# A graph convolution on Trainium2: one indirect gather for each step instead of one for each tile of edges, into fixed buffers

## The reference

```python
# graph part: two layers, with self loops appended to the edges
norm = dis[src] * dis[dst]                 # dis = 1/sqrt(number of edges into a node)
out  = segment_sum((h @ W)[src] * norm[:, None], dst) + b
h    = elu(out)
# mixing part: linear attention over all 6250 rows
q, k = elu(q) + 1, elu(k) + 1
out  = (q @ context) * 1 / max(q . k_sum, 1e-6);   context = k^T v per head
out  = out @ Wproj^T + bproj
x = x + gnn(xn) + mix(xn)
x = x + ffn(layernorm(x))                  # top 2 of 8 experts, gelu, 256 -> 1024 -> 256
```

## Time and profile before

| what | us |
|---|---|
| median of 3 runs | 3484.71 (3480.18 to 3488.33) |
| the profiled execution: its own time | 3488.13 |
| the profiled execution: span in the profile | 3486.4 |
| preparation, 0 to 128.2 | 128.2 |
| layer 0, 128.2 to 1331.3 | 1203.1 |
| dense stage, 1331.3 to 1465.4 | 134.1 |
| layer 1, 1465.4 to 2656.5 | 1191.1 |
| routing and feed-forward part, to the end | 829.9 |

### The profile page before, as it was taken

How to read it: one execution, slowest core, us unless ns; L and a number is a source line. 1 busy time by engine, 2 the same in 40 slices (tenths; PEclk the granted TensorE clock), 3 DMA queues, 4 the chain that set the end, 5 groups by cost and what they waited for, 6 DMA issues and landing times. The chain is left out here.

```text
span 3486.4 us, 52130 instructions
## 1 busy us (share of the span) xinstructions
PE 2318.2 (66%) x12513; PEld 1677.3 (48%) x12513; DVE 1795.5 (52%) x4307; ACT 665.9 (19%) x1375; POOL 2016.0 (58%) x2139
## 2 busy tenths in 40 slices
PE   2156666666666667435556565665668689999998
PEld 2033333443444435323333333333336579999998
DVE  7334444444444445424444444444555756667676
ACT  2200000000000004400000010010103634444343
POOL 2666666666666662566666666666663235555554
PEclk9867777777677778756665567666668789999999
DMA  5544444444444440356666666666661346546551
GB/s 135 176 127 129 132 134 132 132 131 133 131 131 130 131 122 37 108 162 187 178 183 185 185 186 186 185 185 184 183 187 42 128 142 201 166 111 186 143 144 22
DMA packets 202955, 506.69 MB, mean 145 GB/s; under 512 B 42393, under 2 KB 96570, under 8 KB 194538
## 3 DMA queue, kind: packets, MB, share of 16 engines
q0 software_dynamic: 121824, 335.79, 36.1%
q1 hardware_dynamic: 50926, 109.87, 8.8%
q10 hardware_dynamic: 30012, 58.67, 4.8%
HBM read 425.37 MB, written 81.50 MB: 145 GB/s over the span
## 5 line engine op out<-in xcount | busy, mean ns | idle before, releaser
L689 POOL DMA_INDIRECT rows<-rows_layer,srcs x1564 | 1532.8, 980 | 811.2 <-SPq L711 430.1
L740 DVE TENSOR_TENSOR acc<-acc,l_bank 128x256 f32 x1666 | 699.2, 420 | 1301.5 <-PE l_bank L753 554.7
L750 PE MATMUL l_bank<-rows,sel 128*128 x1666 | 578.2, 347 | 722.7 <-SPq L705 319.7
L750 PEld LDWEIGHTS l_bank<-rows,sel 128*128 128x128 bf16 x1666 | 199.3, 120 | 989.8 <-SPq L705 522.5
L752 PE MATMUL l_bank<-rows,sel 128*128 x1666 | 589.3, 354 | 8.9 <-issue 8.8
L753 PE MATMUL l_bank<-rows,sel 128*128 x1666 | 588.5, 353 | 5.5 <-issue 5.5
L1718 PE MATMUL ps_y<-whl,hhi 128*128 128x512 f32 x896 | 320.8, 398 | 0.0
L718 DVE TENSOR_TENSOR sel<-iota_n,dloc 128x512 bf16<-128x512 f32 x418 | 286.3, 685 | 19.2 <-issue 19.2
L1674 POOL DMA_INDIRECT out<-ys,g_sum x112 | 180.3, 1610 | 196.7 <-DVE ys L1630 167.9
L1589 ACT ACTIVATE hr<-ffn_bank,vec 128x256 f32<-128x256 f32 x448 | 212.8, 475 | 372.3 <-PE ffn_bank L1530 333.2
L1528 PE MATMUL ffn_bank<-xh,whl 128*128 128x256 f32 x896 | 252.7, 282 | 2.4 <-DVE xl L1604 2.4
(11 more groups left out here) (285 smaller groups left out, 3126.7 us busy)
## 6 DMA issues: line engine op xcount, KB each, us to landing
whl<-w_hi SPq DMA_DIRECT2D x32, 1024.0 KB
whl<-w_lo SPq DMA_DIRECT2D x32, 1024.0 KB
rows<-rows_layer,srcs POOLq DMA_INDIRECT x1564
w_qkv<-wide ACTq DMA_DIRECT2D x49, 335.0 KB
w_hi<-whi ACTq DMA_DIRECT2D x49, 335.0 KB
w_lo<-wlo ACTq DMA_DIRECT2D x49, 335.0 KB
rows_layer<-part SPq DMA_DIRECT2D x25, 384.0 KB, 2.4
rows_layer<-prep_mem SPq DMA_DIRECT2D x7, 1344.0 KB, 5.2
```

Source lines behind the costliest of these rows:

```text
L689: pool.indirect_dma_start(rows[:, (n + 1) % ROWS, :], None, table[layer], bass.IndirectOffsetOnAxis(ap=srcs[:, n:n + 1], axis=0)).then_inc ...
L740: v.tensor_tensor(to, to, step_bank(s), ALU.add).wait_op(sem(f"summed{layer}"), s + 1, "sem-ge").then_inc(sem(f"added{layer}"), 1)
L750: t.matmul(step_bank(s), sel[:, s % SELS, :], rows_flat[:, bass.ds(slot * DP, D)], start=True, stop=False).wait_op(sem(f"here{layer}"), t. ...
```

## The change

Each step gets a gather of its own, also when two steps share a tile. So step s always finds its rows in slot s % 32, and its slot semaphore has a value that is known when the program is built (`landed`). TensorE's matmuls get constant addresses and wait for the slot's semaphore themselves; its registers and `tiles_of` go. GpSimd waits for `summed` itself, for the step 31 before (s - ROWS + 1). SyncE has no work in the layers any more: `tiles_here` and `steps_until_free` go, with `here` and `freed`. In the preparation the sources are fetched per step like the destinations, by seven indirect gathers on GpSimd; of the three tables of words the blocks' is left. `srcs` has 896 columns instead of 782. VectorE's `step_add` and `blocks_of` stay as they are, but for the table's index.

```diff
-BEHIND, FREED_AT = 16, 8
...
-            word_i = sb(ph, "word_i", [P, 3, SG, 2], U16)
+            word_i = sb(ph, "word_i", [P, SG, 2], U16)
...
-                    full = ET // P * P
-                    sp.wait_ge(sem("copy_s"), 32)
-                    sp.dma_start(rows_i[:, 1, 0:SG - 1, :], e_src_rows[0:full, :].rearrange("(g p) w -> p g w", p=P)
-                                 ).then_inc(sem("rows_s"), 16)
-                    sp.dma_start(rows_i[0:ET - full, 1, SG - 1, :], e_src_rows[full:ET, :]).then_inc(sem("rows_s"), 16)
-                    sp.wait_ge(sem("word_i"), 6)
+                    sp.wait_ge(sem("word_i"), 2)
                     with nc.allow_non_contiguous_dma("small"):
-                        for k in range(3):
-                            sp.dma_start(tab_d[k, :, :].rearrange("(g p) w -> p g w", p=P), word_i[:, k, :, :]
-                                         ).then_inc(sem("word_d"), 16)
+                        sp.dma_start(tab_d[0, :, :].rearrange("(g p) w -> p g w", p=P), word_i[:, :, :]
+                                     ).then_inc(sem("word_d"), 16)
...
+                    pool.wait_ge(sem("copy_s"), 32)
+                    for g in range(SG):
+                        at = bass.IndirectOffsetOnAxis(ap=t_i[:, g:g + 1], axis=0)
+                        pool.indirect_dma_start(rows_i[:, 1, g, :], None, e_src_rows, at).then_inc(sem("rows_s"), 16)
...
-                        v.tensor_scalar(word_i[:, 0, :, k], t_i[:, :], 1.0, None, ALU.add).then_inc(sem("word_i"), 1)
-                        v.tensor_scalar(word_i[:, 1, :, k], b_s[:, :], float(D), None, ALU.mult).then_inc(sem("word_i"), 1)
-                        v.tensor_copy(word_i[:, 2, :, k], tb[:, :]).then_inc(sem("word_i"), 1)
+                        v.tensor_scalar(word_i[:, :, k], b_s[:, :], float(D), None, ALU.mult).then_inc(sem("word_i"), 1)
...
-                    t.wait_ge(sem("rows_f"), 2)
+                    t.wait_ge(sem("rows_f"), 1)
                     for g in range(SG):
-                        n = min(P, ET - g * P)
-                        ins = t.transpose(ps_src[:, g * P:g * P + n], rows_f[0:n, g, :], ident[0:n, 0:n])
+                        ins = t.transpose(ps_src[:, g * P:(g + 1) * P], rows_f[:, g, :], ident[:, :])
...
-                    a.wait_ge(sem("rows_s"), 32)
-                    n = ET % P
-                    a.activation(rows_f[:, 0:SG - 1, :], rows_i[:, 1, 0:SG - 1, :], ACT.Copy).then_inc(sem("rows_f"), 1)
-                    a.activation(rows_f[0:n, SG - 1, :], rows_i[0:n, 1, SG - 1, :], ACT.Copy).then_inc(sem("rows_f"), 1)
-                    for j, (lo, hi) in enumerate(((0, 4 * P), (4 * P, ET))):
+                    a.wait_ge(sem("rows_s"), SG * 16)
+                    a.activation(rows_f[:, :, :], rows_i[:, 1, :, :], ACT.Copy).then_inc(sem("rows_f"), 1)
+                    for j, (lo, hi) in enumerate(ROW_COLS):
...
-            for n in range(ET):
-                if n >= ROWS:
-                    pool.wait_ge(sem(f"freed{layer}"), n - ROWS + 1)
-                pool.indirect_dma_start(rows[:, (n + 1) % ROWS, :], None, table[layer],
-                                        bass.IndirectOffsetOnAxis(ap=srcs[:, n:n + 1], axis=0)
-                                        ).then_inc(sem(f"slot_{n % ROWS}"), 16)
-        def steps_until_free(n):
-            _, regs = nc.values_load_multi_w_load_instructions(
-                words[2:3, n + 1:min(n + FREED_AT, ET - ROWS) + 1, 0], engines=(SP_ENGINE,), min_val=1, max_val=STEPS,
-                skip_runtime_bounds_check_because="the first step of the next tile of edges")
-            return list(regs)
-        def tiles_here(sp, layer):
-            until = []
-            for n in range(ET):
-                sp.wait_ge(sem(f"slot_{n % ROWS}"), (n // ROWS + 1 + layer * -(-(ET - n % ROWS) // ROWS)) * 16)
-                sp.sem_inc(sem(f"here{layer}"), 1)
-                m = n - BEHIND
-                if 0 <= m < ET - ROWS:
-                    if m % FREED_AT == 0:
-                        until = steps_until_free(m)
-                    sp.wait_ge(sem(f"summed{layer}"), until[m % FREED_AT])
-                    sp.sem_inc(sem(f"freed{layer}"), 1)
+            for s in range(STEPS):
+                if s >= ROWS:
+                    pool.wait_ge(sem(f"summed{layer}"), s - ROWS + 1)
+                pool.indirect_dma_start(rows[:, s % ROWS, :], None, table[layer],
+                                        bass.IndirectOffsetOnAxis(ap=srcs[:, s:s + 1], axis=0)
+                                        ).then_inc(sem(f"slot_{s % ROWS}"), 16)
+        def landed(layer, s):
+            return (s // ROWS + 1 + layer * -(-(STEPS - s % ROWS) // ROWS)) * 16
...
-                words[1:2, s:min(s + LOADED, STEPS), 0], engines=(DVE_ENGINE,), min_val=0, max_val=(BLOCKS - 1) * D,
+                words[0:1, s:min(s + LOADED, STEPS), 0], engines=(DVE_ENGINE,), min_val=0, max_val=(BLOCKS - 1) * D,
                 skip_runtime_bounds_check_because="a step's tile is one of the step's number or less, by less than the blocks")
-            return list(regs)
-        def tiles_of(s):
-            _, regs = nc.values_load_multi_w_load_instructions(
-                words[0:1, s:min(s + LOADED, STEPS), 0], engines=(PE_ENGINE,), min_val=1, max_val=ET,
-                skip_runtime_bounds_check_because="a count of tiles, 1 to ET")
             return list(regs)
...
-        def step_sum(t, layer, s, here):
-            slot = t.snap(here & (ROWS - 1))
-            t.to_reg(slot)
+        def step_sum(t, layer, s, rows):
             if s < PSB:
                 t.wait_ge(sem(f"selected{layer}"), s // FOUR + 1)
             else:
                 t.wait_ge(sem(f"added{layer}"), s - PSB + 1)
-            t.matmul(step_bank(s), sel[:, s % SELS, :], rows_flat[:, bass.ds(slot * DP, D)], start=True, stop=False
-                     ).wait_op(sem(f"here{layer}"), t.to_reg(here), "sem-ge")
-            t.matmul(step_bank(s), sel[:, s % SELS, :], rows_flat[:, bass.ds(slot * DP + D, D)], start=False, stop=False)
-            t.matmul(step_bank(s), sel[:, s % SELS, :], rows_flat[:, bass.ds(slot * DP + 2 * D, D)], start=False, stop=True
+            part_of = [rows[:, s % ROWS, k * D:(k + 1) * D] for k in range(3)]
+            t.matmul(step_bank(s), sel[:, s % SELS, :], part_of[0], start=True, stop=False
+                     ).wait_op(sem(f"slot_{s % ROWS}"), landed(layer, s), "sem-ge")
+            t.matmul(step_bank(s), sel[:, s % SELS, :], part_of[1], start=False, stop=False)
+            t.matmul(step_bank(s), sel[:, s % SELS, :], part_of[2], start=False, stop=True
                      ).then_inc(sem(f"summed{layer}"), 1)
...
-        def tensor_steps(t, layer, between):
-            tiles = tiles_of(0)
+        def tensor_steps(t, layer, rows, between):
             for s in range(STEPS):
-                step_sum(t, layer, s, tiles[s])
-                if s % LOADED == 1 and s + LOADED - 1 < STEPS:
-                    tiles.extend(tiles_of(s + LOADED - 1))
+                step_sum(t, layer, s, rows)
                 if s < NT * TURN:
                     between(s // TURN, s % TURN)
...
-                @block.sync
-                def _(sp):
-                    tiles_here(sp, 0)
```

More of the change, by code:

```diff
@@ L38 @@
 TURN = 16
-BEHIND, FREED_AT = 16, 8
-assert ROWS > BEHIND and ROWS & (ROWS - 1) == 0 and PAD_DST + NT < 1 << 16 and BLOCKS * D < 1 << 16 and ET < 1 << 16
+assert PAD_DST + NT < 1 << 16 and BLOCKS * D < 1 << 16 and ET < 1 << 16
 HEADS, HD = 8, 32
@@ L108, in gps_layer @@
     e_src = dram("edges_src", [ET * P, 1], I32)
-    tab_d = dram("step_words", [3, SG * P, 2], U16)
+    tab_d = dram("step_words", [1, SG * P, 2], U16)
     table = [dram(f"rows_layer{i}", [n * P, DP], BF16) for i, n in enumerate((NT, 2 * PAIRS))]
@@ L154, in gps_layer @@
         dloc = sb(steps_ctx, "dloc", [P, SG * P])
-        srcs = sb(steps_ctx, "srcs", [P, ET], I32)
-        words = sb(steps_ctx, "words", [3, SG * P, 2], U16)
+        srcs = sb(steps_ctx, "srcs", [P, SG * P], I32)
+        words = sb(steps_ctx, "words", [1, SG * P, 2], U16)
         ctx_q = sb(steps_ctx, "ctx_q", [P, KC, D])
@@ L431, in _ @@
                     sp.dma_start(node[0:TAIL, NT - 1, :], x[(NT - 1) * P:N, :]).then_inc(sem("x_last"), 16)
-                    sp.wait_ge(sem("word_d"), 48)
+                    sp.wait_ge(sem("word_d"), 16)
                     sp.dma_start(words[:, :, :], tab_d).then_inc(sem("words"), 16)
@@ L789, in gps_layer @@
             rows = sb(ph, "rows0", [P, ROWS, DP], BF16)
-            rows_flat = rows[:, :, :].rearrange("p r d -> p (r d)")
             sel = sb(ph, "sel0", [P, SELS, P], BF16)
@@ L889, in between @@
                             ins.then_inc(sem("m_kv"), 1)
-                    tensor_steps(t, 0, between)
+                    tensor_steps(t, 0, rows, between)
                     t.matmul(ps_c[:, 0:D], zero[:, 0:P], zero[:, 0:D], start=False, stop=True, skip_group_check=True)
```

(5 more changed lines are left out.)

## The result

| | before | after |
|---|---|---|
| median of the runs, us | 3483.68 (3480.18 to 3488.33, 4 runs) | 3554.5 (3552.9 to 3557.97, 4 runs) |
| ratio to before, 95% interval | | 1.0204 (1.0186 to 1.0221) |
| span in the profile, us | 3486.4 | 3551.2 |

The kernel became 70.8 us slower. The forecast was slower by 131 us, with 3385 to 3660 us as the range. So the direction is right, the time lies in the range, and the step is little more than half of what was forecast.

A forecast was written before the change was run, and what follows sets the result against it. The bound was a chain with waits, GpSimd's gathers and late TensorE signals throttling each other. From 3488.1 us profiled, +130 for gathers and +1 for preparation gave 3619, a median of 3616 us; range 3385 to 3660.

The forecast's parts named there:

- The pace goes with the gathers, not the steps: Both layers: gathers keep 1.47 to 1.50 us each while a step shrinks from 1.49 to 1.39 us.
- 51 gathers a layer at 1.28 us, +130: GpSimd in both layers: each added gather costs its unstalled 1.28 us, +65 us a layer.
- The stalls stay what they are: GpSimd's waits on the full ring, 0.22 and 0.20 us per gather, keep their sum after the change.
- the relay: SyncE passing landings to TensorE and sums to GpSimd; removal taken as 0, at most 0.22 and 0.20 us per gather.
- TensorE's registers: 209 register loads of 0.987 us per layer plus address arithmetic; removal taken as 0, at most 0.25 us a step.
- The forecast's own sign: Profile after: 833 gathers per layer, first and last start some 1225 to 1250 us apart, stalls about 0.2 us each.
- The pace of 1.481 at the start of layer 0: Stretch with one gather per step, 200 / 135 us, taken for all 833 gathers: +60 us in layer 0.
- Two parties throttling each other: Layers: gathering GpSimd delays TensorE's signals, late sums fill the ring, GpSimd stops, signals get through; stalls 0.22 and 0.20 us.
- The 7 us that I read off: Layer 0: VectorE's add of 149.01 was read as 7 us behind its matmul.
- Preparation +1: Before the layers: seven more gathers against fewer stores and VectorE operations, +1 us, bounds -5 and +6.
- partial relief: Layers: the shorter chain shortens stalls, 1.37 us per step, -33 and -19, 3434 us; chance 0.20.
- No lateness any more: Layers: direct waits end GpSimd's full-ring stalls, 1.28 us a gather, -108 and -94, about 3284 us; chance 0.10.

The follow-up runs named there:

- before_again: The kernel before, unchanged, run again with a profile on a third chip, one without stalls: 3117.8 us.
- after_again: The changed kernel, unchanged, run again beside the kernel before on a chip without stalls: 3235.47 us, 1.0366 of before.
- gathers_782: The changed kernel with 782 gathers per layer again, spread over 833 steps, output wrong: 3098.06 us, 0.9931 of before.
- plain_loads: The changed kernel with each step's 128 rows loaded by a plain SyncE DMA of consecutive rows, no GpSimd gathers: 2582.0 us, chip with stalls.
- three_stores: The changed kernel with the table of words stored three times instead of once: 3535.39 us, where before took 3460.95.
- registers: The changed kernel with TensorE's register loads, address arithmetic and dynamic addresses put back, with two stores of words: 3238.48 us, 1.0379 of before.

## Why the prediction came out as it did

First the two comparisons of spans, from the first and last start of each layer's gathers (us):

| | chip of the result | chip without stalls (before_again, after_again) |
|---|---|---|
| preparation | -4.8 | -5.6 |
| layer 0, first to last gather | 1172.1 to 1208.2: +36.1 | 1004.9 to 1060.4: +55.5 |
| layer 0, behind the last gather | 30.8 to 25.6: -5.2 | 6.8 to 5.3: -1.5 |
| dense stage | 134.2 to 131.2: -3.0 | 132.9 to 137.2: +4.3 |
| layer 1, first to last gather | 1159.1 to 1206.9: +47.8 | 1006.3 to 1070.8: +64.5 |
| layer 1, behind the last gather | 31.3 to 25.3: -6.0 | 6.8 to 5.0: -1.8 |
| the rest | -0.2 | +3.5 |
| span | +64.8 | +118.9 |

- **The pace goes with the gathers, not the steps: right where nothing stalls.** gathers_782 took away 102 gathers, and 130 us went from the layers. With stalls it wasn't tried, and there 102 more gathers cost 84 us.
- **51 gathers a layer at 1.28 us, +130: right as the price of a gather, wrong as the whole.** Where GpSimd doesn't stall, the gathers cost +120 (55.5 + 64.5), 1.18 us each, and 1.28 us is the interval itself. On the chip of the result they cost +84.
- **The stalls stay what they are: the step that failed.** The forecast took 0 for the relay and 0 for TensorE's registers. The interval fell from 1.501 to 1.452 and from 1.484 to 1.451 us: over 832 gathers that is -40 and -28 us, and behind the last gather another -5 and -6. The bound given for it (the whole stall, 0.22 and 0.20 us a gather) held, and the true value is some 0.05 and 0.03 of it: about a fifth. The forecast's own sign, 1225 to 1250 us from first to last gather, failed with it, at 1208 and 1207. What part of the diff brought the relief isn't settled. Relay and registers were each put back, but only on chips without stalls, where neither moves the time by more than 6 us.
- **The pace of 1.481 at the start of layer 0 as the pace of the layer after: failed with it.** That stretch had one gather per step, but also the relay and the register loads; I used it as if only the ratio counted. The changed kernel runs 200 / 138 = 1.449 there.
- **Two parties throttling each other: right for that chip.** After the change finished sums still wait up to 31 us for their adds, and plain_loads shows the lateness gone without the gathers. The 7 us that I read off were the interval from one add to the next: the add of 149.01 is that of the sixth sum, 7.8 us behind it, and the eighth waits 24 us. But I took it for how a gathering GpSimd works. On three other chips GpSimd gathers without a stop and the signals are prompt, so the reading holds for the chip that it was taken from and is no rule.
- **Preparation +1: wrong in sign, inside its bounds.** -4.8 us, all of it from the stores (three_stores), and one of the two fewer would have done (registers). The seven new gathers cost nothing: their conversion starts at 37.92 us, where it had been 38.62. (The forecast's 44.4 us for that conversion was also added up too high: by its own terms it is 43.5 to 43.8, which makes the upper bound +5; nothing hangs on it.)
- **Of the rivals,** partial relief was the nearest: its mechanism, a shorter stall, is what happened, at 1.45 us and not at its 1.37, and so without its sign. "No lateness any more" came about as a property of a chip, and then the change costs more, not less: the kernel before isn't late either.

## What to carry to other kernels

When GpSimd issues indirect gathers one after the other, count them first: a 128-row gather took GpSimd 1.28 us here where it didn't stall, with 1536 bytes a row and with 512, and a scheme that makes addresses constant by gathering more often paid 1.18 us for each more where nothing stalled and 0.82 us where the gathers stalled. A price for a wait that two engines share (a stall per gather) shouldn't be carried over when the hand-over behind it changes; give the change in the hand-over a value between its bounds, not the end that says nothing happens. Pair a signal with its reader by counting steps, not by what stands next to each other in a timeline. And where a wait is far longer than the work it waits for, look at the same program on a second chip before explaining it by the program.

## What the runs showed of the hardware that was not expected

- The same program has two paces: 3461 to 3484 us in two groups of runs and 3118 to 3119 us in three, on other chips. For the kernel before, the spans differ by 370.3 us, and 368.6 of them lie between the first gather and the last add of the two layers; the part behind layer 1 takes 830.5 in both. The granted clock doesn't explain it: for the changed kernel it is 0.762 on the slower chip and 0.756 on the faster one.
- On the slower chips TensorE's completion signals reach VectorE up to 31 us late while GpSimd gathers; when SyncE's DMAs bring as many bytes, no add starts more than 3.3 us behind its sum. On the others they are prompt while GpSimd gathers.
- An indirect gather of 128 rows keeps GpSimd for 0.98 us with 1536 bytes a row and for 0.98 us with 512.
- Three stores of words at 17 us instead of one or two delay the seven gathers issued around them by some 5 us (33.1 to 35.2 us, for 28.4 to 29.9).
- Loads of the same size, of consecutive rows, issued as plain DMAs by SyncE run at 0.83 us a step and 229 GB/s; gathered by GpSimd, 136 GB/s on a chip with stalls and 155 on one without.
- Not tried: the kernel before with one store of words fewer, which by registers should give it back those 5 us (its three tables need three stores as they stand); eight sums in flight on a chip with stalls; relay, registers and gathers of fewer bytes there. No version that beats both kernels was found.
